# Edge phase of a two-layer graph network: feature loads on ScalarE's queue, all count fills in one run, counts scattered four groups behind

## The reference, cut to what matters

```python
# block 0: messages over the edges, summed at idx_i = src
x_i = ssp(xa @ W_i.T + b_i); x_j = ssp(xa @ W_j.T + b_j)
msg = x_j[idx_j] * (f_ij @ W_att.T)            # idx_j = dst, f_ij = edge_attr_16
m = x_i + segment_sum(msg, idx_i)
...                                            # 3 residual layers, gate, W_v
x = layernorm(x + block0)
# block 1: two attention layers over the same edges, 2 heads
alpha = (q[dst] . k[src]) / 8
a = softmax of alpha over the edges of one dst
h = segment_sum(a * v[src]) averaged over heads + x @ ws + bs
x = layernorm(x + block1)
```

## Time and profile before

| | us |
|---|---|
| median of 3 runs | 4406.83 |
| the runs | 4406.09 to 4412.79 |
| the profiled execution | 4409.64 |
| its span, first to last instruction | 4407.8 |

### The profile page before, as it was taken

The page is one execution under the profiler, slowest core; times in us unless marked ns, Lnnn a source line. Parts: engine busy times, 40 slices in busy tenths (PEclk is TensorE's granted clock), DMA queues, the critical chain, the costliest instruction groups (busy, mean ns, idle before and its releaser), DMA issues.

```text
span 4407.8 us, 66127 instructions
## 1 busy us (share of the span) xinstructions
PE 3359.4 (76%) x18324; PEld 2081.7 (47%) x18324; DVE 3038.8 (69%) x9485; ACT 947.1 (21%) x1947; POOL 3007.5 (68%) x2211
## 2 busy tenths in 40 slices
PE   4687878787878877877788773477677776999996
PEld 3455555555555555555555542233333334555554
DVE  4567666666666666666666652487777777888886
ACT  2000000000000000000000022355455554333333
POOL 3268888888888888888888865155454635488885
PEclk7899889888988898889889886799999998999997
DMA  8211111111111111111211111233233231222221
GB/s 320 87 12 13 13 13 13 13 13 13 13 13 13 13 13 13 13 13 13 13 13 13 12 6 0 70 89 84 84 84 89 82 89 53 64 69 65 69 64 29
DMA packets 301248, 194.46 MB, mean 44 GB/s; under 512 B 147296, under 2 KB 281977, under 8 KB 301177
## 3 DMA queue, kind: packets, MB, share of 16 engines
q1 hardware_dynamic: 158391, 166.55, 12.9%
q0 software_dynamic: 137984, 26.19, 10.6%
q10 hardware_dynamic: 4802, 0.98, 0.1%
HBM read 112.88 MB, written 80.67 MB: 44 GB/s over the span
## 4 chain that ended last, share of the span: by engine, by line
POOL 40%; issue 25%; DMA 18%; PE 7%; DVE 5%; SPq 3%; ACT 2%; POOLq 0%; ACTq 0%; DVEq 0%
POOL edge_counts L391 16%; POOL x_nodes L382 13%; POOL scores L430 11%; DMA edge_counts<-small 8%; DMA log_counts<-counts_and_logs 6%; PE PS L1105 3%; DMA edge_counts<-scores 2%; DVE scores L885 2%; SPq L293 2%; PE PS L1013 1%; DMA counts_and_logs<-edge_counts 1%; PE PS L1095 1%; PE PS L1118 1%; DVE counts_and_logs L874 1%; ACT scores L597 1%
## 5 line engine op out<-in xcount | busy, mean ns | idle before, releaser
L1013 PE MATMUL PS<-scores 128*128 128x320 bf16 x11760 | 1844.8, 322 | 507.1 <-DVE scores L767 500.6
L1013 PEld LDWEIGHTS PS<-scores 128*128 128x128 bf16 x11760 | 1224.5, 105 | 1139.4 <-DVE scores L767 516.8
L430 POOL TENSOR_TENSOR scores<-scores,max_of_targets 125x484 f32<-125x484 f32 x626 | 942.5, 1542 | 635.2 <-ACT max_of_targets L614 635.2
L391 POOL DMA_INDIRECT edge_counts<-small x720 | 1160.2, 1611 | 243.3 <-issue 243.3
L382 POOL DMA_INDIRECT x_nodes<-xj_rows,small x784 | 794.4, 1013 | 376.4 <-issue 189.6
L1095 PE MATMUL PS<-q_chunk,k_features 128*125 128x484 f32 x1300 | 650.9, 594 | 233.0 <-DVE scores L885 230.8
L728 DVE SCALAR_TENSOR_TENSOR scores<-PS,small,scores 128x256 bf16<-128x256 f32 x784 | 332.9, 481 | 713.1 <-PE PS L993 623.7
L1105 PE MATMUL PS<-scores,v_nodes 125*65 125x242 f32 x2600 | 668.7, 386 | 118.6 <-ACT scores L597 116.9
L767 DVE TENSOR_SCALAR scores<-scores,small 128x192 bf16<-128x192 bf16 x3920 | 747.0, 297 | 6.1 <-issue 2.5
L1105 PEld LDWEIGHTS PS<-scores,v_nodes 125*65 125x65 f32 x2600 | 359.2, 143 | 528.3 <-ACT scores L597 257.9
L896 DVE TENSOR_TENSOR running_max<-running_max,scores 125x484 f32<-125x484 f32 x624 | 544.3, 872 | 21.5
(11 more groups left out here) (160 smaller groups left out, 1699.2 us busy)
## 6 DMA issues: line engine op xcount, KB each, us to landing
edge_counts<-counts_and_logs SPq DMA_DIRECT2D x50, 768.5 KB
counts_and_logs<-edge_counts SPq DMA_DIRECT2D x325, 118.2 KB
log_counts<-counts_and_logs SPq DMA_DIRECT2D x325, 118.2 KB
counts_and_logs<-log_counts SPq DMA_DIRECT2D x325, 118.2 KB
x_nodes<-xj_rows,small POOLq DMA_INDIRECT x784
edge_counts<-small POOLq DMA_INDIRECT x720
scores<-in_edge_attr_dram SPq DMA_DIRECT2D x97, 48.0 KB
scores<-in_edge_attr_dram SPq DMA_DIRECT2D x97, 16.0 KB
```

Source lines behind the costliest of these rows:

```text
L391: pool.indirect_dma_start(cnt_dram, bass.IndirectOffsetOnAxis(ap=index[:, s:s + 1], axis=0), value[:, s:s + 1], None, compute_op=ALU.add). ...
L430: nc.gpsimd.tensor_tensor(Tt[:, b, i], Tt[:, b, i], MB, ALU.subtract).then_inc(sem("shifted"), 1)
L1013: ins = nc.tensor.matmul(PS[:, b, 0:HI * F], onehot[:, s, b * P:b * P + 128], spread[:, s, i].rearrange("p h f -> p (h f)"), start=first a ...
```

## The change

It has three parts. (1) `load_features` for groups 2 to 97 is issued by ACT: the load of group 2 right behind the copy of group 0's turned features, that of group g + 3 at the end of ACT's `edge_group(g)`, behind the copy of group g + 1's. (2) SP issues the 50 fills without the wait for `xj_stored`. (3) `BEHIND` is 4: groups 0 to 3 only gather, groups 4 to 97 gather and scatter, the tail has the scatters of 4 groups.

```diff
-EARLY_FILLS = 8
-BEHIND = 8
+BEHIND = 4
...
             for a in range(FILLS):
-                if a == EARLY_FILLS:
-
-                    sp.wait_ge(sem("xj_stored"), 32)
                 sp.dma_start(cnt_fills[:, a, :], cfill).then_inc(sem("counts_cleared"), 16)
...
-            def load_f(g, u):
-                sp.wait_ge(sem("fT_in_psum"), g - 1)
-                load_features(sp, g, u)
-
-
-            with sp.Fori(1, NG // 2 - 1) as k:
-                for u in range(2):
-                    load_f(2 * k + u, u)
-            for u in range(2):
-                load_f(NG - 2 + u, u)
...
             copy_fT(0)
+            load_features(act, 2, 0)
             for u in range(2):
                 edge_group(u, False)
-            with act.Fori(1, NG // 2 - 1) as k:
+                load_features(act, u + 3, 1 - u)
+            with act.Fori(1, NG // 2 - 2) as k:
                 for u in range(2):
                     edge_group(2 * k + u, False)
-            for u in range(2):
-                edge_group(NG - 2 + u, u == 1)
+                    load_features(act, 2 * k + u + 3, 1 - u)
+            for u in range(4):
+                edge_group(NG - 4 + u, u == 3)
+                if u == 0:
+                    load_features(act, NG - 1, 1)
```

## The result

| | us |
|---|---|
| before, median of 4 runs | 4408.3 (4406.1 to 4412.8) |
| changed, median of 4 runs | 4354.4 (4351.0 to 4354.9) |
| ratio, 95% interval | 0.9875 (0.9858 to 0.9892) |
| forecast | 4324 (4302 to 4352) |

The change gains 54 us where 83 were forecast, and ends 2.4 us above the range. In a later comparison on another occasion it measured 4347.2 (4341.2 to 4350.6) against 4405.4, ratio 0.9863 (0.9848 to 0.9878).

The account below looks back on a forecast made before the run. POOL's loop (25.89 us a group) was taken to bound the kernel, its end set by its start. First scatter 85.3 + 62.7 = 148.0; gain 230.8 - 148.0 = 82.8; 4409.6 - 82.8 = 4326.8, so forecast 4324 (4302 to 4352).

Parts of the forecast that it names:

- product of group 0: DVE's first product, behind ACT's store and weight issues: moves by 12.2 + 1.4 + 8.1 = 21.7 us, from 63.61 to 85.3.
- from it to the first scatter: Start of POOL's loop: 25.5 + 24.1 us to group 2's product, then 13.1 to the first scatter, 62.7 in all.
- loop, 94 groups: POOL's scatters and gathers keep 25.89 us a group, so 94 groups take 2433.7 us.
- end of loop to first logarithm: ACT's q comes 118.1 us behind the loop's end; node layers, not counts, end last, and the logarithm follows.
- its two ends: Bounds on the x_j store's delay beside the fills: no cost below, 46.3 us above; a value between was taken.
- The upper end, row by row: x_j store: each of 195 rows per DMA engine waits for one fill row of 0.2375 us, 46.3 us.
- 12.2 us of backlog: x_j store waits only for fills already queued: 6.4 fills of 1.9 us each.
- Rival 2: x_j store against fills, row by row: 46.3 us delay, first scatter 172.6, gain 58.2, time 4349; chance 0.13.
- the shared issue: ACT's and SP's queues take turns on one issuing resource, so SP adds no fills while the store's rows are written.
- Rival 3: x_j store against fills: engines change queues after a dozen or so store rows; 28.5 us, gain 66.5, time 4340; chance 0.10.
- What would show it: Profile signs; wrong if store lands elsewhere than 58 us, loop period moves over 0.1 us, or counts still end last.
- `Wblk`'s term: ACT's eight block-weight transfers, each behind a fill: 8 x 1.9 = 15.2 us against 7.12 before, 8.1 more.

## Why the forecast was wrong

The sum against the profiled execution was 82.8 us, and 58.6 came out:

| term | forecast | measured | share of the miss |
|---|---|---|---|
| product of group 0 | 85.3 | 107.55 | -22.3 |
| from it to the first scatter | 62.7 | 65.9 | -3.2 |
| loop, 94 groups | 2433.7 | 2436.8 | -3.1 |
| end of loop to first logarithm | 118.1 | 116.3 | +1.8 |
| everything behind | as before | 2.6 shorter | +2.6 |

**The step that failed** is the value taken for the store between its two ends. The upper end, row by row, gave 46.3 us; the first gather started 46.0 us later. I took 12.2 us of backlog, because the `Wblk` issues went from 0.61 to 1.40 us beside fills: I read from this that only what is already queued stands in the way. The observation holds (27.8 us for ACT's store, and in the kernel with 3 KB rows 2.57 us for a fill of SP beside it), the conclusion does not: SP's queue held some 6 fills of 8 rows per engine, was topped up while the store drained at the same rate of rows, and so never ran dry. Only where almost no backlog stands, as with 3 KB rows, does the store go through. With it the path changed: the sum had product 0 behind ACT and the gathers covered, and the gathers ended last (107.55 against 85.3).

That 46.0 is so near 46.3 is in part luck. From its first row to its last the store took 46.1 us (42.4 to 88.5) instead of 4.8 (39.4 to 44.2), so the turns cost 41.3 us. The first row came 3.0 us later than before, and from the last row to POOL's first gather it took 1.6 us longer.

The Trainium skill, "Perfetto Trace Analysis", section "DMA Instruction — HWDGE (DVE, Sync)", says that the block is locked for exclusive use until all descriptors of one transfer are generated. That does not describe this case: SP went on issuing fills at 1.8 us each while the longer of ACT's two transfers was being issued for 27.4 us:

```profile
59.70 3.57 SPq L289 DMA_DIRECT2D edge_counts<-counts_and_logs  x2
```

Rival 2 was this mechanism with this price: first scatter 172.6 and a gain of 58.2, against 173.46 and 58.6 in the profiles. Two of its steps miss and cancel: product 0 moved by 43.9 us, not 46.3, and the way from it to the first scatter took 65.9, not 62.7. I gave it 0.13 on the strength of the shared issue. What should have weighed more stood in the earlier trace rows: 3218 packets for 0.81 MB are 252 bytes each, one row of the store, and 153 for 0.84 MB about one row of a fill. If turns go by packets, they go by rows, and nothing in the rows spoke for larger turns.

**Rival 3**, turns of several rows, is out. The Trainium skill, "DMA: Bandwidth & Descriptors", section "Queues, rings and completion order", says that an engine drains a packet of about 9 to 17 descriptors before it turns. Here it turned after each row, by the counts (277 to 277, 191 to 189) and by the order of the starts (242 of 245, 169 of 170). The measurement decides.

**What would show it** gave three signs of being wrong, and one came true: the store landed near 91, not 58. The period, 25.92 here, moved by more than 0.1 only in the later occasions, and there for all kernels alike.

**Right, by the steps:** the loop is POOL's and keeps its period (25.92 against 25.89); the first scatter follows DVE's work on group 2 (160.34 + 13.1 = 173.4); ACT's loads are free under its idle time; the fills of the changed kernel end near 120 us, and nobody waits for them; the tail is 103 us; the node layers become the last to end. With 8 fills ahead instead, the fills do hold the first scatter, by 12 us, which the forecast had no reason to price.

**The size of `Wblk`'s term** was 15.2 us for eight issues and measured 17.2; they began at 65.8 where my sum had 56.2, and were in the end covered by the gathers, for which product 0 still waited 10.65 us.

**The range** ended at 4352, 3 us above rival 2's time; the median of one occasion, 4354.4, lies above it and that of the other, 4347.2, inside. The loop's period does not explain this. It moves by 0.2 us a group (17 us in 94 groups) between these two, but the wrong way, and other parts give it back: in the later occasion's profile the first scatter comes 7.2 us sooner, the loop takes 16.5 us longer, and from the first logarithm to the end it takes 1612.4 us instead of 1622.6, so that the two profiled executions agree (4351.0 and 4350.6). Why these parts move against each other is open.

## What to carry to other kernels

Where two queues both hold work, count rows, not bytes (shown here for SP's queue beside ACT's): a transfer of many short rows beside a stream of long ones pays its rows per engine times the time of a long row, here 195 x 0.24 us for 0.8 MB that takes 6 us alone. Keep such a transfer out of the stream, or give it long rows; the second needs no wait, was 10 us faster than 8 fills ahead on one occasion, and is level with 12 fills ahead on another. And price a part together with the others: the fills in one run cost 5 us alone and 31 to 41 beside the two parts that had removed what covered it.

## What was not expected of the hardware

A queue that is not kept full loses its hold: with rows of 3076 bytes, whose issue (0.95 us for 8 rows per engine) is no faster than their transfer, the store ran at 1046 rows to 70 for 2 us. Halving the fill's row took the delay from 46.0 to 6.5 us, not to 23, in one run. And issuing is charged to the engine: ACT stood 27.8 us in the two instructions of the store and 7.11 us in the first of the small ones behind it, so what stood behind the store in ACT's program waited with it: x_i started 33 us later.

```profile
38.36 27.36 ACTq L477 DMA_DIRECT2D xj_rows<-scores  x1
65.81 7.11 ACTq L482 DMA_DIRECT2D scores<-scores  x1
```
